# Inverse transform of a Fourier layer on TensorE: four 64x64 tiles per step become two 64x128 tiles

## The reference, cut to what matters

```python
for l in range(4):                       # 64 channels, 16 x 16 kept modes at either end
    xf  = rfft2(h)
    top = einsum('bixy,ioxy->boxy', xf[:, :, :16, :16], w1)
    bot = einsum('bixy,ioxy->boxy', xf[:, :, -16:, :16], w2)
    sc  = irfft2(of)                     # of: zeros, with top and bot set in
    pw  = einsum('bihw,oi->bohw', h, pw_w[l]) + pw_b[l]
    y   = sc + pw
    h   = gelu(gamma * (y - mean(y)) / sqrt(var(y) + eps) + beta)
h = gelu(h @ fc1_w + fc1_b); out = (h @ fc2_w + fc2_b).squeeze(-1)
```

## Time and profile before

| | |
|---|---|
| runs | 4116.05, 4126.1, 4130.21 us, median 4126.1 |
| profiled execution | 4140.94 us, span 4139.1 us |
| PE / PEld / DVE / ACT / POOL busy | 3211.6 / 1865.4 / 2414.9 / 2248.7 / 173.7 us |
| MATMUL and LDWEIGHTS instructions | 52,804 each |
| L896 | 16,384 MATMUL (620.0 us busy), 16,384 LDWEIGHTS (558.1 us busy) |
| L905 | 256 transposes, 318.5 us |
| stretches of the fuse, layers 0 to 3 | about 253 to 929, 1106 to 1765, 1944 to 2614, 2793 to 3441 us |

### The profile page before, as it was taken

One profiled execution on the slowest core, in us unless ns is written; L12 is line 12 of the kernel. 1 busy time (PEld: TensorE's weight loads), 2 busy tenths in 40 slices (PEclk: granted clock), 3 DMA queues, 4 the chain that ended last, 5 costly groups with the idle time before them and its releaser, 6 DMA issues. The chain is left out here.

```text
span 4139.1 us, 119258 instructions
## 1 busy us (share of the span) xinstructions
PE 3211.6 (78%) x52804; PEld 1865.4 (45%) x52804; DVE 2414.9 (58%) x2482; ACT 2248.7 (54%) x2652; POOL 173.7 (4%) x249
## 2 busy tenths in 40 slices
PE   6668888886677787865777777676999994869776
PEld 4544444444544444445444444463444442733532
DVE  4555555554577777855777777563333333454556
ACT  3655666664566666655666666564666663222321
POOL 2013200000000000000000000000010011000000
PEclk9889999998899999988999999887999997679688
DMA  8867766769779888997788888975534320012062
GB/s 287 321 186 190 186 158 155 175 153 327 256 219 268 251 258 254 275 313 264 232 248 279 234 248 248 304 268 205 183 125 153 137 85 12 1 42 41 1 115 61
DMA packets 173872, 798.69 MB, mean 193 GB/s; under 512 B 31881, under 2 KB 38353, under 8 KB 124014
## 3 DMA queue, kind: packets, MB, share of 16 engines
q1 hardware_dynamic: 162524, 776.18, 61.6%
q0 software_dynamic: 7936, 13.65, 1.1%
q10 hardware_dynamic: 2898, 1.17, 0.1%
HBM read 446.06 MB, written 342.23 MB: 190 GB/s over the span
## 5 line engine op out<-in xcount | busy, mean ns | idle before, releaser
L896 PEld LDWEIGHTS bank<-fb,arena 64*64 64x64 f32 x16384 | 558.1, 196 | 544.2 <-issue 487.3
L896 PE MATMUL bank<-fb,arena 64*64 64x128 f32 x16384 | 620.0, 290 | 199.1 <-issue 142.6
L913 DVE TENSOR_TENSOR arena<-bank,arena 128x1024 f32<-128x1024 f32 x384 | 467.7, 1218 | 426.0 <-PE bank L896 423.8
L1138 ACT ACTIVATE arena<-bank 128x1024 f32<-128x1024 f32 x384 | 383.6, 1023 | 526.7 <-PE bank L1060 308.0
L905 DVE STREAM_TRANSPOSE arena<-bank 128x1024 f32<-128x1024 f32 x256 | 318.5, 1244 | 374.8 <-PE bank L886 374.5
L1181 DVE STREAM_TRANSPOSE arena<-arena 128x1024 f32<-128x1024 f32 x384 | 458.3, 1212 | 134.9 <-ACT arena L1128 133.0
L1060 PE MATMUL bank<-arena,wst 64*64 64x512 f32 x3072 | 415.1, 624 | 22.5 <-issue 17.8
L886 PE MATMUL bank<-arena,ga 64*64 64x256 f32 x4096 | 299.0, 400 | 147.4 <-DMA arena<-arena 60.8
L1145 ACT ACTIVATE arena<-arena 128x1024 f32<-128x1024 f32 x384 | 403.2, 1050 | 0.3
L1131 ACT ACTIVATE arena<-arena,shift,scale 128x1024 f32<-128x1024 f32 x256 | 316.6, 1237 | 115.7 <-DVE arena L913 114.5
L636 PE MATMUL bank<-arena 64*64 64x128 f32 x8192 | 283.1, 287 | 98.5 <-issue 68.4
(11 more groups left out here) (240 smaller groups left out, 3650.1 us busy)
## 6 DMA issues: line engine op xcount, KB each, us to landing
y_dram<-arena SPq DMA_DIRECT2D x384, 512.0 KB, 8.1
arena<-y_dram SPq DMA_DIRECT2D x96, 2048.0 KB
spec_out<-arena SPq DMA_DIRECT2D x128, 512.0 KB, 11.2
arena<-in_w_modes SPq DMA_DIRECT2D x28, 2048.0 KB, 15.0
arena<-spec_out SPq DMA_DIRECT2D x112, 512.0 KB, 10.9
arena<-spec_in SPq DMA_DIRECT2D x24, 2048.0 KB, 10.2
spec_in<-arena SPq DMA_DIRECT2D x96, 512.0 KB, 7.8
spec_in<-arena SPq DMA_DIRECT2D x8, 2048.0 KB, 13.2
```

Of the source, the lines that this page charges most:

```text
L896: mm = pe.matmul(hpx(bank[2 * s + i][CHAN[v], :])[:, :, j * S:(j + 1) * S], a2[p % 2][CHAN[i], :, v, 4 * T + j], hpx(fb2[CHAN[i], :]), sta ...
L913: dve.tensor_tensor(chunk(p, T), slot(s), chunk(p, T), ALU.add).then_inc(y_added, 1)
L1138: act.activation(chunk(p, T), slot(NEXT_SLOT[T]), ACT.Copy).then_inc(evicted, 1)
```

## The change

`a2` becomes `[2, C, M1]`: image half, channel, row in the half. `turn_rows` writes through a rearranged view so that each 32-element block of its output lands as two runs of 16. The 128 columns (half, channel) for one row are then evenly 16 elements (64 bytes) apart, and `spectral` loads them as one 64x128 operand; the loop over v goes, and the tile position is `(i * C, 0)`.

```diff
-        a2 = [at(2 * PX + u * PX // 2, C, 2, M1) for u in range(2)]
+        a2 = [at(2 * PX + u * PX // 2, 2, C, M1) for u in range(2)]
...
                 for i in range(2):
-                    for v in range(2):
-                        mm = pe.matmul(hpx(bank[2 * s + i][CHAN[v], :])[:, :, j * S:(j + 1) * S],
-                                       a2[p % 2][CHAN[i], :, v, 4 * T + j], hpx(fb2[CHAN[i], :]),
-                                       start=(alone or j == 0), stop=alone, tile_position=(i * C, v * C))
+                    mm = pe.matmul(hpx(bank[2 * s + i])[:, :, j * S:(j + 1) * S],
+                                   a2[p % 2][CHAN[i], :, :, 4 * T + j].rearrange("p a c -> p (a c)"), hpx(fb2[CHAN[i], :]),
+                                   start=(alone or j == 0), stop=alone, tile_position=(i * C, 0))
...
-            dve.transpose(a2[p % 2].rearrange("p (v c) a m -> p v (c a m)", v=2)[:, :, hc * 512:(hc + 1) * 512],
-                          slot(s)).then_inc(rows_turned, 1)
+            dve.transpose(a2[p % 2].rearrange("p a (v c) m -> p v c a m", v=2)[:, :, hc * 16:(hc + 1) * 16],
+                          slot(s).rearrange("p v (c a m) -> p v c a m", a=2, m=M1)).then_inc(rows_turned, 1)
```

## The result

The changed kernel takes 4328.6 us (median of 4 runs, 4300.3 to 4340.7) against 4128.2 us for the kernel before (4 runs, 4116.1 to 4137.9): a ratio of 1.050, with a 95% interval of 1.046 to 1.054. It is 200 us slower. The profiled execution took 4338.3 us with a span of 4336.5.

The account below looks back on a forecast made before the run. TensorE was taken to set the pace, its L896 blocks bound by stationary-operand loads. First layer 137, layers 1 and 2 102 and last layer 58 sum to 297 us; on 4126.1 that gives 4423, said as 4420, range 4060 to 4530.

Parts of the forecast that it names:

- The load: L896 blocks: loading 128 spread columns takes 0.22 us a round instead of 0.115, so a block grows by 0.84 us.
- The first rival: L896 rounds: the load doesn't double, staying about 190 ns, so the kernel gets faster, 4072 us; chance 0.16.
- Closeness, not exact distance: Operand loads: columns that aren't close cost double, 64 bytes apart like 128, about 1.8 ns per column.
- The change of tile shape: TensorE's block boundaries: each change of tile shape between neighbouring blocks costs 0.15 us.
- First layer: First layer's fuse: one chain without cover, so 4.3 us a pair over 32 pairs, +137 us.
- Last layer: Last layer's fuse: four dearer blocks less a gap and five shape changes, 1.8 us a pair, +58 us.
- VectorE: The 256 transposes writing runs of 16 elements: taken as 0 added, upper bound +0.92 us each.
- The rival that had them at 2.17 us: VectorE's transposes get slower, L904 at 2.17 us, while the loads don't double: 4236 us; chance 0.05.
- Layers 1 and 2: Middle layers' fuses: 3.0 us a pair less what stalls give back, 1.6 x 64 = +102 us, between 0 and 190.
- I take 1.4 of 3.0 as given back: Middle layers: fewer instructions over longer time recover 1.4 us a pair of some 3.5 us of instruction-fetch stalls.
- the last rival: Middle layers: the instruction prefetch absorbs their whole cost, leaving 4126 + 195 = 4321 us; low end of the main case.

Follow-up runs that it names:

- e3: Changed kernel, but the 64x128 operand reads 128 neighbouring elements, other values than the product needs: 4071.5 us against 4113.0 for the kernel before, ratio 0.992.
- e10: Changed kernel with columns 8 bytes apart and the transpose split in two, first layer in 64x64 tiles: 4048.2 us against 4109.4 before, ratio 0.984.
- e8: Changed kernel with the 64x128 operand's columns 8 bytes apart and the transpose split in two: 4099.7 us against 4109.4 before, ratio 0.996.
- e7: Changed kernel with the 128 columns contiguous and right, transposes writing single elements 512 bytes apart: 4102.9 us, ratio 1.001 to the kernel before.
- e5: Kernel before, with the 2 MB loads of L866 reading one block in eight (layers 1 to 3): 3976.6 us, a single run.
- e6: Changed kernel, with the 2 MB loads of L866 reading one block in eight (layers 1 to 3): 4250.3 us, a single run.
- e4: Kernel before, but each 64x64 operand reads 64 neighbouring elements, so other products: 4117.0 us, ratio 1.003.
- e9: Kernel before, with the columns of its 64x64 operand 8 bytes apart, one transpose as before: 4123.0 us against 4122.1, ratio 1.001.
- e11: Changed kernel with four rows interleaved, columns 16 bytes apart, transpose in two instructions: 4382.8 us, a single run.

## Why the prediction was right, and where it was off

I forecast 4420 us and slower; it is 4329 and slower, inside the range and 91 us below its middle. Step by step:

- **The load.** Forecast: 0.22 us a round, a median near 300 ns, blocks of 1.8 to 2.1 us. Measured: 308 ns, which less the 80 ns of latency is 0.228 a round, and blocks of 1.95 us. That the spacing does it is shown by e3 (188 ns, all else equal). The first rival, a load that doesn't double, falls with it.
- **Spacing, not distance.** "Closeness, not exact distance" held: 128 bytes 195 ns and 64 bytes 198 for 64 columns; 16 bytes 326 and 64 bytes 308 for 128; 8 bytes 135 and 193, contiguous 133 and 188. By the Trainium skill (SBUF — State Buffer, Specifications) a line has 16 bytes and needs two hits for full bandwidth: two fp32 columns share a line at 8 bytes and none at 16, and there the step lies. Its rule for loads (TensorE: Matmul & The Clock Gate, LDWEIGHTS), the number of columns over 1.2 GHz, gives 53 ns for 64 more columns; the contiguous loads agree (188 - 133 = 55) and the spread ones don't (308 - 195 = 113).
- **The change of tile shape.** Forecast 0.15 us; e10 against e8 shows 0.16 ahead of a block. That was right; behind a block it isn't shown by itself.
- **First layer.** Forecast +137; measured +135.3. At full clock a pair grew from 20.13 to 24.49 us, 4.36 against the 4.3 forecast. That the whole agrees so well is partly luck: half clock, which the forecast left out, costs the changed kernel some 10 us more here, by the prices read above (22 pairs of 31 have such a stretch instead of 6), and the start of the layer and a few longer pairs of the kernel before make up for it.
- **Last layer.** Forecast +58; measured +49.0 (a pair 20.90 instead of 19.25 us: 1.65, where I had 1.8). Its blocks grew by less than 0.84, since where L1315 stands ahead, the load hides behind it:

```profile
3292.74 1.13 PE L1315 MATMUL bank<-arena,fc 64*128 64x512 f32 x4
3293.68 1.82 PE L895 MATMUL bank<-fb,arena 64*128 64x128 f32 x16
3295.32 1.05 PE L1315 MATMUL bank<-arena,fc 64*128 64x512 f32 x4
```

  That block takes 1.64 us (3295.32 - 3293.68), against 1.13 for its like of before: +0.51.
- **VectorE.** Forecast 0; the transposes' median is 1250 ns in both. The rival that had them at 2.17 us falls. e7 shows that single elements would cost 1977 ns each, and would show as some 34 us.
- **Layers 1 and 2.** This is the term that was mis-sized: +102 forecast, +10.3 measured. The step is "I take 1.4 of 3.0 as given back". Two things were off. The undisturbed pair grew by 2.42 us, not 3.0: y2 by 0.57 (0.46 + 0.11), where I had 0.73, y3 by 0.78, where I had 0.99 (the wait behind it took back some), and y0 and y1 by 1.06, where I had 1.3. The greater part is what comes back: of the 75 us of a layer, 66 and 74. The stalls inside blocks are 54 and 60 us shorter from start to start, 46 and 52 by the idle time alone; the half clock behind the stalls is worth some 20 more. The forecast had the stalls and named their cause, but not what they do to the clock. I had bounded the term rightly (none to all) and chose in the middle; it came out at the end, as in the last rival, "the prefetch absorbs it all in the middle layers". The 200 us measured lie near the 195 that this end had.

What gives it back is shown in part. That it hangs on the DMA traffic is shown by e5 and e6: with the traffic thinned the change costs 42 and 48 us a layer, 33 and 46 more than with it (a single run of each). That it is the instruction fetch, and not the data, rests on the form of the stalls (inside blocks where nothing is waited for, all 63 ending 1.2 to 1.6 us behind a packet), on VectorE's hardly waiting for the data, and on e3 and e8, where a fifth fewer matmuls and loads nearly halve them. By the Trainium skill (Runtime: NRT & Kernel Launch, Instruction fetch mechanics) a sequencer fetches blocks of 256 instructions on its own DMA queue, and the cost of crossing into the next one is mostly hidden; the blocks' size agrees with the earlier trace rows, but at a DMA share of 0.85 the fetch isn't hidden: 81 us of the 659 of layer 1's stretch were such stalls. A packet that has begun is as quick as elsewhere; why it begins late beside the data is open, and no run tells.

## What to carry to other kernels

Before widening a stationary operand, look at the spacing of its columns: fp32 columns 16, 64 or 128 bytes apart load at half speed here, which four tiles side by side all but hide behind the stream and two wide ones don't. Laying two passes' columns beside each other (8 bytes apart) gives the wide tile its load at full speed, and the wide tile then pays where instructions come late beside the data, and where its neighbours have the same shape, but not among other shapes. A cost worked out from an undisturbed pair is an upper bound in a layer that also stalls for instructions: there a slower pace is mostly time in which the next packet comes, and with the stalls goes part of the time at half clock.

## What the runs showed that I had not expected

- **The clock in the first layer.** The granted clock over the first layer's stretch is 0.94 where it was 0.97. In 22 of the 31 pairs a stretch at half clock begins 0.2 to 2.5 us after the 2.37 us of idle time ahead of y0, in the kernel before in 6, near the end of the same idle time; this is one, by busy time in the changed kernel (L1032 takes 1.76 us in it, not 1.09):

```profile
696.00:699.00 3.00, 3.00 (x20) 1.39 (x21) 0.03 (x1) 0.39 (x1) 0.00 (x0) 0.68 0.01 4
```

  0.68 is a mean of the two levels, 1.2 and 2.4 GHz. Such pairs take 25.2 to 25.5 us instead of 24.49; the mean of the layer is 769.7 / 31 = 24.8. Why the slower kernel has more of them is open.
- **The longest loads.** A load of 128 contiguous columns takes 335 ns at most (e3), one of 128 spread columns 311 (changed kernel); with 64 columns both end at 228. These are loads at 1.2 GHz, as the clock's records show: the loads that lie wholly in stretches at half clock have medians of 330 ns contiguous (e3) and 307 spread (changed kernel), against 188 and 308 at full clock, and with 64 columns 227 either way, as the prediction had presumed. So half clock doesn't slow a spread load of 128 columns, and a stretch at half clock costs the changed kernel 0.7 to 1.0 us where it costs the kernel before 1.4 to 1.7.
- **Sixteen bytes are dearer than 64**, 326 against 308 ns a load and 4383 against 4329 us in all, though e11's transposes cost no more than e8's.
- **Cheaper loads that bring nothing.** Loads 62 ns shorter, 16384 of them, moved the time by nothing that can be measured (e4, e9), and a pair by 0.25 us, as the stream of the moving columns stood right behind them.
